# The first expert layer routed over 80 pairs of gathered 128-row blocks, with a per-batch cross-attention behind it

## What is computed

```python
for layer in (0, 1):
    x = x + tanh(g_xattn[layer]) * attend(layernorm(x), ctx)   # layer 0: 16 heads, sliding window of 64
    x = x + tanh(g_ffn[layer]) * moe(layernorm(x))             # layer 1: similarity matrix, softmax, W_qv
# layer 0 experts: 32 of inner size 128; each token uses 8 of them (best 4 of 8 groups, then top 8) and 1 shared
#   expert e: w[t, e] * (silu(x @ Wg.T) * (x @ Wu.T)) @ Wd.T
# layer 1 experts: 8 of inner size 256; each token uses 2 of them, and 2 shared ones
```

## Time and profile before

| what | us |
|---|---|
| median of 3 runs | 1261.09 |
| lowest, highest | 1257.96, 1261.67 |
| the profiled execution, its own time | 1263.34 |
| its span, first to last instruction | 1261.3 |
| mean granted TensorE clock | 0.947 |

### The profile page before, as it was taken

How to read it: one execution, slowest core, us unless ns; L and a number is a source line. 1 busy time by engine, 2 the same in 40 slices (tenths; PEclk the granted TensorE clock), 3 DMA queues, 4 the chain that set the end, 5 groups by cost and what they waited for, 6 DMA issues and landing times.

```text
span 1261.3 us, 21618 instructions
## 1 busy us (share of the span) xinstructions
PE 1093.0 (87%) x6948; PEld 916.5 (73%) x6948; DVE 840.9 (67%) x1991; ACT 484.7 (38%) x947; POOL 334.8 (27%) x371
## 2 busy tenths in 40 slices
PE   3368888877999999999999999988999898799930
PEld 3357777756888888888888888874667586588820
DVE  6679999977676767677777767686645378433323
ACT  5469898942333333333333333323222332122200
POOL 6146565441211111011111111012201232333245
PEclk9789999988999999999999999997999999899975
DMA  8830000010000000000000000620100300122324
GB/s 237 194 80 2 0 0 0 1 52 1 26 25 25 25 16 22 25 25 25 25 25 25 25 13 24 254 68 17 34 17 1 116 1 1 50 85 86 87 88 133
DMA packets 28386, 61.72 MB, mean 49 GB/s; under 512 B 4688, under 2 KB 13392, under 8 KB 28208
## 3 DMA queue, kind: packets, MB, share of 16 engines
q1 hardware_dynamic: 24928, 51.77, 13.8%
q0 software_dynamic: 3408, 9.31, 2.7%
HBM read 42.85 MB, written 9.31 MB: 41 GB/s over the span
## 4 chain that ended last, share of the span: by engine, by line
PE 71%; DVE 16%; issue 5%; DMA 3%; POOL 2%; SPq 1%; ACT 1%; DVEq 0%; POOLq 0%; ACTq 0%
PE bank L763 28%; PE bank L780 14%; PE bank L1140 6%; DVE ptl L557 4%; PE bank L1712 3%; PE bank L1647 3%; PE bank L1161 3%; DVE nmax L549 2%; PE bank L1697 2%; PE bank L1078 2%; PE bank L367 2%; POOL yg L1451 1%; SPq L1995 1%; DMA yg<-y_rows,slot 1%; PE bank L1094 1%
## 5 line engine op out<-in xcount | busy, mean ns | idle before, releaser
L906 DVE SCALAR_TENSOR_TENSOR x<-bank,cw,x 128x256 f32<-128x256 f32 x528 | 218.2, 476 | 5.1 <-PE bank L780 5.1
L763 PE MATMUL bank<-xh,wh 128*128 128x512 f32 x528 | 208.1, 394 | 0.0
L763 PE MATMUL bank<-xl,wh 128*128 128x512 f32 x528 | 207.6, 393 | 0.0
L763 PE MATMUL bank<-xh,wl 128*128 128x512 f32 x528 | 205.9, 390 | 0.0
L982 POOL TENSOR_TENSOR wl<-wraw,wh 128x768 fp32r<-128x768 f32 x33 | 61.0, 1848 | 445.7 <-ACT wh L832 445.7
L852 ACT ACTIVATE hidh<-hid 128x512 fp32r<-128x512 f32 x132 | 83.4, 632 | 213.0 <-DVE hid L917 209.4
L780 PE MATMUL bank<-wh,hidh 128*128 128x256 f32 x528 | 150.8, 286 | 10.5 <-POOL hidl L992 5.3
L780 PE MATMUL bank<-wh,hidl 128*128 128x256 f32 x528 | 151.3, 286 | 0.0
L780 PE MATMUL bank<-wl,hidh 128*128 128x256 f32 x528 | 151.1, 286 | 0.0
L923 DVE TENSOR_TENSOR hidl<-hid,hidh 128x512 fp32r<-128x512 f32 x124 | 85.9, 693 | 86.6 <-ACT hidh L852 86.6
L845 ACT ACTIVATE sil<-bank 128x512 f32<-128x512 f32 x132 | 79.1, 599 | 163.6 <-PE bank L763 163.6
(11 more groups left out here) (222 smaller groups left out, 2076.5 us busy)
## 6 DMA issues: line engine op xcount, KB each, us to landing
wraw<-in_w SPq DMA_DIRECT2D x37, 384.0 KB, 3.1
kst<-khl SPq DMA_DIRECT2D x32, 224.0 KB, 6.0
wres<-in_w SPq DMA_DIRECT2D x4, 1536.0 KB, 16.6
y_rows<-yb SPq DMA_DIRECT2D x39, 128.0 KB
x<-in_x SPq DMA_DIRECT2D x4, 512.0 KB, 8.0
craw<-in_ctxt SPq DMA_DIRECT2D x4, 512.0 KB, 4.8
traw<-in_ctx SPq DMA_DIRECT2D x4, 512.0 KB, 4.7
xn_rows<-xn SPq DMA_DIRECT2D x4, 512.0 KB, 4.8
```

What stands on the lines that cost most here:

```text
L763: mm = pe.matmul(o[:, :], wp[:, par, w], xp[:, c, b * SEQ:(b + 1) * SEQ], start=(n == 0), stop=(n == 5))
L906: op = nc.vector.scalar_tensor_tensor(out=x[:, t, :], in0=bank[4 + 2 * vp + j // 2][:, (j % 2) * DIM:(j % 2 + 1) * DIM], scalar=w, in1=x[: ...
```

## The change

The experts of layer 0 become sparse in the way those of layer 1 are, in blocks of 128 gathered rows. 16 tiles by 8 experts need 128 blocks if all were full; with up to one unfilled block for each expert the list is 160 long (`BLOCKS0`). It is worked through in 80 pairs (`PAIRS0`). A block has one expert of inner size 128 and float32 weights; all 33 experts' weights stay in SBUF (`wres0`), loaded in four DMAs (12.4 MB in all). The fp32r split of layer 0 is gone. The shared expert is still applied to all tokens, in float32, on PE, ACT and POOL.

- Before the pairs run, the logits, the choice of experts, the ranks, the places and the one-hot matrices are made one after another. For each of 16 tiles DVE compares 1024 and 1280 float16 elements (`hot`), ACT multiplies 1024 by the token's number, and PE sums 8 products (`ids`).
- In the pairs DVE copies the transposed rows and makes the hidden values, ACT does silu and the other two copies, POOL issues two gathers a pair, and SP stores 256 KB a pair.
- The results of layer 0 are combined inside the cross-attention stage: 8 gathers a tile, 128 in all, on POOL, and 8 dependent additions a tile on DVE, four tiles a batch.
- The cross-attention has single buffers, and a batch starts on PE when the one before is through. `aenc` and the scaling of `prob1` move from DVE to ACT, and the bias becomes a matmul with one row.

The core of the diff; functions of layer 1 otherwise change in semaphore counts alone.

```diff
-NB0 = SH0 + E0
+BLOCKS0 = TILES * TOP0 + E0
+PAIRS0 = BLOCKS0 // 2
+W0_GROUPS = ((0, 1), (1, 9), (9, 17), (17, 33))
...
+            for i in range(PAIRS0):
+                es = [pe.value_load(expi0[0:1, 2 * i + s:2 * i + s + 1], min_val=0, max_val=E0 - 1) for s in range(2)]
+                gate_up(i, 0, es[0])
+                if i:
+                    hidden_transposed(i - 1)
+                if i + 1 < PAIRS0:
+                    rows_transposed(i + 1)
+                gate_up(i, 1, es[1])
+                if i:
+                    down(i - 1, was)
...
+            def hot(t):
+                nc.vector.tensor_tensor(rowhot0[:, t % 2], countk[:, 1:P + 1, :],
+                                        rowk0[:, t:t + 1, :].broadcast_to([P, P, TOP0]), ALU.is_equal)
+                nc.vector.tensor_tensor(blkhot0[:, t % 2], countk[:, :, :],
+                                        blkk0[:, t:t + 1, :].broadcast_to([P, BLOCKS0, TOP0]), ALU.is_equal)
...
+            for i in range(PAIRS0):      # moe0_sync
+                sp.wait_ge(r1["ys"], i + 1)
+                sp.dma_start(y_rows0[...], yb0[:, i % YS])
+                if i == 60:
+                    sp.wait_ge(m.rs, STEPS0)
+                    parameters_a1(sp)
+                    sp.dma_start(rraw[:, :, 0:E1], rw1_in).then_inc(moe.rload, 16)
+                    sp.dma_start(rbias[:, :], rbias1_in.broadcast_to([P, E1])).then_inc(moe.rload, 16)
+                    context_load(sp, 0)
+                    context_load(sp, 1)
...
             for b in range(BATCH):       # tensor_a1
+                transposes(b)
+                scores(b)
+                maxima_row(b)
                 probs_transposed(b, (0, 1))
+                maximum_spread(b)
+                probs_transposed(b, (2, 3))
+                attended(b)              # sum_spread(b) inside
                 context_bar(b)
                 output(b)
...
+            for t in range(TILES):       # pool_a1
+                gathers(t)
+                if t >= TPB and t % TPB == 0:
+                    ln_rsqrt(pool, 2, t // TPB - 1)
+                if t >= TPB and t % TPB == 1 and t // TPB >= 2:
+                    ln_rsqrt(pool, 3, t // TPB - 2)
```

More of the change, by code:

```diff
@@ L741, in logits_by_token @@
                 pe.wait_ge(m.ltc, b + 1)
[L742 to L752, removed]
-                if late(v, 2):
-                    pe.wait_ge(m.sil, v - 1)
-                for half, ready in ((0, m.gate), (1, m.up)):
-                    if half == 1 and late(v, 2):
-                        pe.wait_ge(m.h, v - 1)
-                    o = bank[2 * half + vp]
-                    n = 0
-                    for c in range(CH):
-                        w = slice((CH * half + c) * FF, (CH * half + c + 1) * FF)
-                        for wp, xp in ((wh, xh), (wh, xl), (wl, xh)):
-                            mm = pe.matmul(o[:, :], wp[:, par, w], xp[:, c, b * SEQ:(b + 1) * SEQ],
-                                           start=(n == 0), stop=(n == 5))
-                            n += 1
-                    mm.then_inc(ready, 1)
@@ L1638, in transposes, with scores @@
                     mm.then_inc(A["tr"], 1)
-            def scores(b, tiles):
+            def scores(b):
                 pe.wait_ge(A["a"], 2 * b + 2)
                 pe.wait_ge(A[f"ctx_t{b % 2}"], 16 * (b // 2 + 1))
-                for j in tiles:
+                for j in range(TPB):
                     if 4 * b + j >= 2:
@@ L1709, in output @@
                         for j in (half, half + 2):
+                            o = bank[4 + half][:, (j // 2) * DIM:(j // 2 + 1) * DIM]
+                            if g == 0:
+                                pe.matmul(o, ones[0:1, :], bqv[0:1, :], start=(j == half), stop=False,
+                                          skip_group_check=True)
+                                continue
                             for c in range(CH):
-                                w = wqv[:, CH * g + c, :] if g else w14[:, c, :]
@@ L1712, in output @@
-                                mm = pe.matmul(bank[4 + half][:, (j // 2) * DIM:(j // 2 + 1) * DIM],
-                                               feats[:, c, j * P:(j + 1) * P], w, start=(g == 0 and c == 0 and j == half),
-                                               stop=(g == 2 and c == CH - 1), skip_group_check=True)
+                                w = wqv[:, CH * (g - 1) + c, :] if g > 1 else w14[:, c, :]
+                                mm = pe.matmul(o, feats[:, c, j * P:(j + 1) * P], w, start=False,
+                                               stop=(g == 3 and c == CH - 1), skip_group_check=True)
@@ L1768, in row_exp, with probs_copy @@
                                      accum_out=ebs[:, :]).then_inc(A["eb"], 1)
[L1770 to L1773 removed]
+            def probs_copy(b):
+                for jc in range(TPB):
                     act.wait_ge(A["pt"], 4 * b + jc + 1)
@@ L1816, in row_terms, with maxima @@
                                                    accum_out=rterm[:, j:j + 1]).then_inc(A["r"], 1)
[L1818 to L1827 removed]
+            def maxima(b):
+                for j in range(TPB):
                     dve.wait_ge(A["sim"], 4 * b + j + 1)
```

1287 lines of the change are left out of this document (695 added, 592 removed), and 4 rows, old and new, of the table s_a1.

## The result

The changed kernel takes 1201.15 us (median; 1198.83 to 1209.87) against 1261.07 before: a ratio of 0.954, 95% interval 0.950 to 0.959. I had said 1180 with a range of 1125 to 1240. The time lies 21 us above the forecast, and the parts behind it missed by more, in both directions.

A forecast was written before the change was run, and what follows sets the result against it. TensorE's matmuls were taken to bound layer 0's experts and the cross-attention; experts −234 us and cross-attention +153 gave −81 in all. The cross-attention ending at 901 plus 278.8 unchanged gave 1180 us, range 1125 to 1240.

The forecast's parts named there:

- the rival that ended slower: Pairs: POOL's gathers stretched beside DVE, two taking 5.3 us, pairs 424 in place of 260; +164, 1344 us; chance 0.05.
- the wait at pair 60: Pairs: SP's 3.1 MB of parameters and contexts between the stores make TensorE wait 6 us, bounds 0 and 15.
- TensorE idle for 47 us: Sign, between the last pair and the first cross-attention batch: TensorE has nothing to do for 47 us.
- The register loads: Pairs: two loads need 0.9 us, hidden behind the 0.87 down product; put at nothing, bound 0.4 a pair (+32).
- The lists: Layer 0 before the pairs: sixteen tiles of one-hot matrices at 1.6 us each, 26 plus 1; bounds 18 and 43.
- the shared expert: Layer 0 before the pairs: 21 us beside DVE's chain, put at nothing; at half clock holds third tile's comparison up to 4.
- The comparisons keep the pace of float32: Rival on the lists' tiles: 43 us in place of 26, +17, 1197 us; chance 0.12.
- my byte count: Lists: 1024 float16 elements are as many bytes as 512 float32 ones, hence 1.6 us a tile.
- Ahead of the lists: Layer 0 before the one-hot tiles: norm, logits, expert choice, weights and places, from 262.4 to 303.8.
- The batches: Cross-attention: 60 us a batch, half speed for somewhat under half of the passes; the last batch 57.
- the chain at full clock: Cross-attention: one batch's dependent steps, through the fourth combination, take 48.4 us at full clock.
- The two rivals on the clock: Cross-attention: clock stays up, −47, 1133 us, chance 0.16; half clock through the whole stage, +63, 1243 us, chance 0.16.

The follow-up runs named there:

- e1_split: Changed kernel with the register load for a pair's second block moved ahead of that block's gate and up product: 1178.96 us, ratio 0.938 to the kernel before.
- e9_warm: e1_split with token weights made behind the tiles, loads spread over the pairs, and 7 idle products in TensorE's two pauses ahead of the list products: 1163.9 us, one run.
- e4_fill: Changed kernel with 7 idle float32 products of 512 columns on TensorE behind each of the first three cross-attention batches: 1204.2 us in one run.

## Why the prediction was right, and where it was not

The frame held: TensorE's busy time in the experts' stage fell from 573 to 370 us, and what came in front and behind was what the prediction named. No gather was stretched as the rival that ended slower needed: the 160 in the pairs took 0.94 (median; 1.23 the longest), and the two of a pair came 1.25 apart. From the last pair to the statistics of the first batch the forecast was right to 1 us, and the wait at pair 60 to 0.7. TensorE's whole wait ahead of that batch was 57.05, where "TensorE idle for 47 us" stood among the signs: that number ends about where the first batch's rows have landed, and the prediction's own chain, with the last additions, the root and the norm, comes to 56. Four terms were off.

- **The register loads** were put at nothing with a bound of 0.4 a pair. They cost 0.36, 29 us, nearly the bound. The step that failed is "TensorE still has the down product of 0.87 to work on": two loads take 0.9 on its queue and the next product has to be issued behind them. The near row of before had one load a block, and one costs next to nothing; two in a row don't. The other terms of the pairs nearly cancelled: the stop took 2.7 more than its 6 with the slow passes behind it, the slow start and the drain some 2 less than their 7.4.
- **The lists.** Forecast 27 for the sixteen tiles, measured 43. I priced the comparisons (1.6 a tile; 1.34 measured) and ACT's pass (1.11; 1.15), and never the eight products, which pace it at 2.32: 37 of the 43. The other 5.7 pass between the first comparison (309.4) and the first product (315.1). There the shared expert, put at nothing with up to 4 for this hold, kept the third tile's comparison for 2.60, since ACT made `rowt` only behind the shared expert's last passes (TensorE, ACT and DVE of the changed kernel, below). "The comparisons keep the pace of float32" was the rival I set against my choice; the tile did come near 2.7, but by another engine. The Trainium skill, "VectorE: DVE Perf Modes", section "The perf-mode tier table (the rule you actually need)", was right where my byte count was not quite: its factor of two gave 1.35.
- **Ahead of the lists** 5.6 more, but only in this execution: the transposes and logits ran wholly at the lower clock in it (262.3 to 282.5; in e1_split 264.2 to 276.7). That explains most of why it lies 8.7 us above the median. From the stage's first transposes to the first comparison it took 47.2 us; e1_split, the same program up to the pairs, took 37.9, 3.5 less than forecast. In both, DVE's steps of 0.69 took longer beside POOL's products and additions for the shared expert, here up to 1.74 (DVE and POOL, below).

```profile
309.96 3.26 PE L834 MATMUL bank<-wres,shid 128*128 128x256 f32 x8
313.85 2.18 ACT L981 ACTIVATE rowt<-rowhot,token 128x1024 f16<-128x1024 f16 x2
315.02 1.07 DVE L1117 TENSOR_TENSOR rowhot<-countk,rowk 128x1024 f16<-128x1024 f16 x1 [2.60 <-ACT rowt L981]
...
293.13 1.74 DVE L1063 TENSOR_TENSOR maskb<-rep,msc 128x512 bf16<-128x512 f32 x1
...
293.05 2.94 POOL L1202 TENSOR_TENSOR x<-x,sy 128x512 f32<-128x512 f32 x2
```

- **The batches** were put 5.3 too long each. What the clock takes is 6.4 and not 11.6: transposes 0.9, scores 2.1 and the first products of the output 3.4, against the same passes at the upper level. Without it 48.3 are left of the 54.7, so the chain at full clock, 48.4, comes out right, though no run had a whole batch at that level. I took half speed for nearly half of the passes from the earlier trace rows; the trace has it for the first 8 us of a batch (772.2 to about 780) and some 7 later on (801 to 807).

Against the median of 1201 the misses are smaller at one place: with e1_split's 86.7 for the stretch up to the pairs they are +10, +28, −1, −20 and +2, which leaves 19 of the 21 us. That the sum came so near is partly luck, since a loss of 38 and a gain of 20 stood against each other. The two rivals on the clock, full and half throughout, were both wrong; the truth lay between them, nearer to full.

## What to carry to other kernels

When a loop takes over a body that runs without a gap, count what is issued on the busiest engine's queue besides its matmuls: one register load between two products cost next to nothing here, two in a row did not, and they could be moved apart for 0.03 us a pair. When a step is handed round three engines, price it on all three, and look at how far apart each reads and writes its elements. Where a chain has slack on an engine, put the additions that nobody waits for there, ahead of the step that the chain needs next.

## What the runs showed that was not expected

- A product of 128x160 float16 with its operands 16 bytes apart takes 0.29 us at clock 1.00 and at 0.50; with both side by side 0.13, at clock 0.50. Under such products the granted clock came down from 1.00 (up to 310 in e9_warm) to 0.50 (from 315 on), though TensorE is never idle in the records.
- DVE's two-input comparison of 1024 float16 elements: 0.60 from start to start with the output in order, 4.3 with it written 256 bytes apart.
- A stop of 8.05 us cost 10.4 in e1_split, the difference being slow passes behind it.
- In e4_fill the clock stayed at 1.00 through pauses of 3.7 to 3.8 us and fell only when TensorE was at work again or just through with it, 1 to 2 us later.
